# An attention kernel's probabilities-times-values product split into bf16 parts, and its projection batched by four row chunks

## The reference

```python
h = jnp.einsum('bse,end->bsnd', layernorm(x), proj_weight)     # 16 heads of 64
q = jnp.einsum('bsnd,ndh->bsnh', h, attn_weight)
scores = jnp.einsum('bsnh,brnh->bsnr', q, h) / head_dim
w = jax.nn.softmax(scores, axis=-1)
v = jnp.einsum('brnd,ndh->brnh', h, value_weight)
attn_out = jnp.einsum('bsnr,brnh->bsnh', w, v)
x = x + attn_out.reshape(b, s, -1) @ out_w.T + out_b
x = x + ffn(layernorm(x))      # gated, quantised weights and activations
```

## Time and profile before

| | us |
|---|---|
| time before, median of 2 runs | 8653.41 (8594.0 and 8712.82) |
| the profiled execution | 8581.15 |
| its span (slowest core, core 7) | 8579.6 |
| the eight cores' spans | 8538.1 to 8579.6 |
| mean granted TensorE clock of the cores | 0.771 to 0.775 of full |
| busy: PE, DVE, ACT | 5091.8, 2980.7, 1585.7 |

### The profile page before, as it was taken

How to read it: one execution, slowest core, us unless ns; L and a number is a source line. 1 busy time by engine, 2 the same in 40 slices (tenths; PEclk the granted TensorE clock), 3 DMA queues, 4 the chain that set the end, 5 groups by cost and what they waited for, 6 DMA issues and landing times.

```text
span 8579.6 us, 85041 instructions; the slowest of 8 cores (8538.1 to 8579.6 us)
## 1 busy us (share of the span) xinstructions
PE 5091.8 (59%) x26150; PEld 2254.4 (26%) x26150; DVE 2980.7 (35%) x7376; ACT 1585.7 (18%) x2602; POOL 88.2 (1%) x134
## 2 busy tenths in 40 slices
PE   0016668778778766668788687785344454353453
PEld 0015522222222215522222222122223232232232
DVE  5666631111111126631211212113543434435434
ACT  0000023333333320023233233231000000000000
POOL 0000000000000000000000000000000000000000
PEclk9997778888888887779889888786656666566566
DMA  8741100000000001100000000003334443343343
GB/s 273 234 143 35 33 7 2 4 2 2 4 2 1 2 19 35 36 9 1 5 2 1 5 2 1 2 1 67 66 80 83 74 89 65 68 94 69 74 89 69
DMA packets 837267, 396.21 MB, mean 46 GB/s; under 512 B 803939, under 2 KB 804067, under 8 KB 830692
## 3 DMA queue, kind: packets, MB, share of 16 engines
q1 hardware_dynamic: 827044, 353.00, 17.7%
q0 software_dynamic: 9792, 37.78, 1.2%
HBM read 352.95 MB, written 33.55 MB: 45 GB/s over the span
## 4 chain that ended last, share of the span: by engine, by line
PE 55%; DVE 23%; DMA 8%; issue 7%; DVEq 6%; ACT 0%; SPq 0%; POOLq 0%; ACTq 0%; POOL 0%
PE pb_av L718 23%; PE pb_s L735 10%; PE pb_av L464 6%; PE pb_av L843 3%; PE pf_d L1364 3%; PE pf_u L1191 2%; PE pf_g L1186 2%; PE pf_d L1191 2%; PE pf_d L1186 2%; DMA f_wd<-wdq 2%; DVE ln_lo L481 2%; DVE ln_hi L479 2%; DVE f_guq L1337 1%; DVE f_gr L1328 1%; DVE f_mx L1214 1%
## 5 line engine op out<-in xcount | busy, mean ns | idle before, releaser
L759 ACT ACTIVATE w<-pb_s,cbias 128x512 f32<-128x512 f32 x2048 | 1296.8, 684 | 1397.2 <-PE pb_s L735 1396.7
L768 DVE RECIPROCAL rr_t<-pb_av 1x512 f32<-1x512 f32 x64 | 210.1, 3320 | 2848.3 <-PE pb_av L718 2848.3
L718 PE MATMUL pb_av<-w,vA 128*65 128x512 f32 x2048 | 1125.4, 632 | 0.0
L718 PE MATMUL pb_av<-w,vB 128*65 128x512 f32 x2048 | 1055.5, 597 | 0.0
L1364 PE MATMUL pf_d<-f_guq,f_wd 128*128 128x256 bf16 x2048 | 299.0, 321 | 642.2 <-DVE f_guq L1337 542.9
L735 PE MATMUL pb_s<-q_hi,h_hi 64*128 64x512 bf16 x2048 | 439.2, 400 | 72.0 <-ACT w L759 71.5
L718 PEld LDWEIGHTS pb_av<-w,vB 128*65 128x65 f32 x2048 | 287.3, 140 | 617.5 <-issue 617.5
L735 PE MATMUL pb_s<-q_lo,h_hi 64*128 64x512 bf16 x2048 | 432.0, 393 | 0.0
L735 PE MATMUL pb_s<-q_hi,h_lo 64*128 64x512 bf16 x2048 | 431.2, 392 | 0.0
L1364 PEld LDWEIGHTS pf_d<-f_guq,f_wd 128*128 128x128 bf16 x2048 | 232.6, 115 | 710.2 <-issue 652.1
L1186 PE MATMUL pf_g<-f_xqf,f_wg 128*128 128x256 bf16 x1024 | 204.1, 366 | 276.3 <-DVEq L1219 267.2
(11 more groups left out here) (211 smaller groups left out, 5911.2 us busy)
## 6 DMA issues: line engine op xcount, KB each, us to landing
f_wg<-wgq SPq DMA_DIRECT2D x256, 256.0 KB, 3.3
f_wu<-wuq SPq DMA_DIRECT2D x256, 256.0 KB, 3.9
f_wd<-wdq SPq DMA_DIRECT2D x64, 1024.0 KB, 8.1
wraw<-wgT SPq DMA_DIRECT2D x16, 2048.0 KB, 10.1
wraw<-wuT SPq DMA_DIRECT2D x16, 2048.0 KB, 10.0
wraw<-wdT SPq DMA_DIRECT2D x64, 512.0 KB, 4.3
xa<-x_full SPq DMA_DIRECT2D x64, 512.0 KB, 3.8
x_tm<-x_full SPq DMA_DIRECT2D x16, 512.0 KB, 13.6
```

The source lines that it names most:

```text
L718: last = te.matmul(pb_av[2 + hidx][0:65, 0:512], vb[:, rc * 66:rc * 66 + 65], w32[:, wofs:wofs + 512], start=(rc == 0), stop=(rc == NRC - 1))
L759: a_e.inc(sc.activation(w32[:, slot:slot + 512], pb_s[hidx][:, 0:512], AFT.Exp, bias=cbias[:, hidx:hidx + 1], scale=1.0 / 64))
L768: v.reciprocal(rr_t[64:65, hidx * 512:(hidx + 1) * 512], pb_av[2 + hidx][64:65, 0:512])
```

## The change

Three edits.

- **AV in bf16 pairs.** vA and vB become bf16 pairs vA_hi, vA_lo, vB_hi, vB_lo: the V stage casts, drains and subtracts, with a one in the hi part's column 64 and a zero in the lo part's. Each exp tile (w32) is split by DVE into w_hi and w_lo, and AV is three bf16 matmuls per head in the place of one f32 matmul. AV waits for DVE's split (`v_w`) where it waited for the exp (`a_e`); the exp's wait for its slot is now on the split of rc - 2 (`v_w`) and no longer on its AV.
- **The projection of h takes four row chunks at once.** ln_hi and ln_lo hold four chunks. The PE does the transposes of four chunks and then 96 matmuls of 512 columns; the split of the first chunk of the next four waits for the whole projection. The h split handles 512 columns at a time and stands, in DVE's order, after the split of the second chunk of the next four.
- The buffer of the squares (xsq) exists once, and ACT drains after each Square.

```diff
-        vA = asb("vA", [128, NRC * 66], F32)
-        vB = asb("vB", [128, NRC * 66], F32)
+        vA_hi = asb("vA_hi", [128, NRC * 65], BF16)
+        vA_lo = asb("vA_lo", [128, NRC * 65], BF16)
+        vB_hi = asb("vB_hi", [128, NRC * 65], BF16)
+        vB_lo = asb("vB_lo", [128, NRC * 65], BF16)
...
-            xsq = hsb("xsq", [128, 2 * E], F32)
+            xsq = hsb("xsq", [128, E], F32)
             lnt = hsb("lnt", [128, E], F32)
-            ln_hi = hsb("ln_hi", [128, E], BF16)
-            ln_lo = hsb("ln_lo", [128, E], BF16)
+            ln_hi = hsb("ln_hi", [128, 4 * E], BF16)
+            ln_lo = hsb("ln_lo", [128, 4 * E], BF16)
...
                 a_sq.inc(sc.activation(
-                    xsq[:, (rc % 2) * E:(rc % 2 + 1) * E],
+                    xsq[:, 0:E],
                     xa[:, (rc % 2) * E:(rc % 2 + 1) * E], AFT.Square,
                     accum_out=stat[:, c + 0:c + 1]))
+                sc.drain()
...
-            def emit_pj(te, rc):
-                v_ls.w(te, bvls + 8 * rc + 8)
+            def emit_pj(te, rcq):
+                v_ls.w(te, bvls + 32 * rcq + 32)
                 for lc in range(4):
-                    pid = rc * 4 + lc
+                    pid = rcq * 4 + lc
...
                             last = te.matmul(
-                                pp[:, 0:128],
+                                pp[:, 0:512],
                                 wop[:, ic * 512 + lc * 128:ic * 512 + (lc + 1) * 128],
-                                rop[:, ic * 128:(ic + 1) * 128],
+                                rop[:, ic * 512:(ic + 1) * 512],
                                 start=first, stop=(wop is pw_lo and ic == 7))
...
-                    if ib == 0 and rc >= 1:
-                        t_pj.w(v, btpj + 4 * rc)
+                    if ib == 0 and rc >= 4:
+                        t_pj.w(v, btpj + 4 * (rc // 4))
                     src = ltp[ib % 4][:, 0:128]
-                    v.tensor_copy(ln_hi[:, ib * 128:(ib + 1) * 128], src)
+                    dst = ib * 512 + (rc % 4) * 128
+                    v.tensor_copy(ln_hi[:, dst:dst + 128], src)
                     v.drain()
...
-                    dst = lc * 4096 + rc * 128
-                    v.tensor_copy(h_hi[:, dst:dst + 128], pp[:, 0:128])
+                    dst = lc * 4096 + rcq * 512
+                    v.tensor_copy(h_hi[:, dst:dst + 512], pp[:, 0:512])
                     v.drain()
                     v_he.inc(v.tensor_tensor(
-                        h_lo[:, dst:dst + 128], pp[:, 0:128],
-                        h_hi[:, dst:dst + 128], ALU.subtract))
+                        h_lo[:, dst:dst + 512], pp[:, 0:512],
+                        h_hi[:, dst:dst + 512], ALU.subtract))
                     v.drain()
...
-                for rc in range(NRC + 1):
-                    if 1 <= rc:
-                        emit_pj(te, rc - 1)
-                    if rc < NRC:
-                        emit_lt(te, rc)
+                v_af.w(te, prev_af_h)
+                for rc in range(NRC):
+                    if rc >= 4 and rc % 4 == 0:
+                        emit_pj(te, rc // 4 - 1)
+                    emit_lt(te, rc)
+                emit_pj(te, NRC // 4 - 1)
...
-                for rc in range(NRC + 2):
+                for rc in range(NRC + 3):
...
-                    if 2 <= rc < NRC + 2:
-                        emit_he(v, rc - 2)
+                    if rc >= 6 and (rc - 6) % 4 == 0:
+                        emit_he(v, (rc - 6) // 4)
...
                 for rc in range(NRC):
                     t_v.w(v, btv + rc + 1)
-                    for (hp, vb) in ((0, vA), (64, vB)):
+                    o = rc * 65
+                    for (hp, vh, vl) in ((0, vA_hi, vA_lo), (64, vB_hi, vB_lo)):
                         pav = pb_av[(0 if hp == 0 else 2) + rc % 2]
-                        v.tensor_copy(vb[:, rc * 66:rc * 66 + 64], pav[:, 0:64])
-                        v.memset(vb[:, rc * 66 + 64:rc * 66 + 65], 1.0)
+                        v.tensor_copy(vh[:, o:o + 64], pav[:, 0:64])
+                        v.memset(vh[:, o + 64:o + 65], 1.0)
+                        v.drain()
+                        v.tensor_tensor(vl[:, o:o + 64], pav[:, 0:64],
+                                        vh[:, o:o + 64], ALU.subtract)
+                        v.memset(vl[:, o + 64:o + 65], 0.0)
                     v_ve.inc(v.drain())
...
                     def emit_av(rc):
                         for hidx in range(2):
-                            a_e.w(te, bae + 2 * rc + hidx + 1)
+                            v_w.w(te, bvw + 2 * rc + hidx + 1)
...
-                            vb = [vA, vB][hidx]
-                            last = te.matmul(
-                                pb_av[2 + hidx][0:65, 0:512],
-                                vb[:, rc * 66:rc * 66 + 65],
-                                w32[:, wofs:wofs + 512],
-                                start=(rc == 0), stop=(rc == NRC - 1))
+                            vh, vl = [(vA_hi, vA_lo), (vB_hi, vB_lo)][hidx]
+                            o = rc * 65
+                            for k, (vv, ww) in enumerate(
+                                    ((vh, w_hi), (vh, w_lo), (vl, w_hi))):
+                                last = te.matmul(
+                                    pb_av[2 + hidx][0:65, 0:512],
+                                    vv[:, o:o + 65],
+                                    ww[:, wofs:wofs + 512],
+                                    start=(rc == 0 and k == 0),
+                                    stop=(rc == NRC - 1 and k == 2))
                         t_av.inc(last)
...
                             if rc >= 2:
-                                t_av.w(sc, btav + rc - 1)
-                            elif btav > 0:
-                                t_av.w(sc, btav + rc - 1)
+                                v_w.w(sc, bvw + 2 * rc - 2)
+                            elif bvw > 0:
+                                v_w.w(sc, bvw + 2 * rc - 2)
...
+                @blk.vector
+                def _(v):
+                    for rc in range(NRC):
+                        for hidx in range(2):
+                            a_e.w(v, bae + 2 * rc + hidx + 1)
+                            slot = (2 * (rc % 2) + hidx) * 512
+                            v.tensor_copy(w_hi[:, slot:slot + 512],
+                                          w32[:, slot:slot + 512])
+                            v.drain()
+                            v.tensor_tensor(w_lo[:, slot:slot + 512],
+                                            w32[:, slot:slot + 512],
+                                            w_hi[:, slot:slot + 512], ALU.subtract)
+                            v_w.inc(v.drain())
```

More of the change, by code:

```diff
@@ L338, in emit_hbuild @@
             prev_nm = v_nm.n
+            prev_af_h = v_af.n
             @blk.sync
@@ L475, in emit_ls, with emit_he @@
                     t_lt.w(v, btlt + tid + 1)
-                    if ib == 0 and rc >= 1:
-                        t_pj.w(v, btpj + 4 * rc)
+                    if ib == 0 and rc >= 4:
+                        t_pj.w(v, btpj + 4 * (rc // 4))
                     src = ltp[ib % 4][:, 0:128]
-                    v.tensor_copy(ln_hi[:, ib * 128:(ib + 1) * 128], src)
+                    dst = ib * 512 + (rc % 4) * 128
+                    v.tensor_copy(ln_hi[:, dst:dst + 128], src)
                     v.drain()
                     v_ls.inc(v.tensor_tensor(
-                        ln_lo[:, ib * 128:(ib + 1) * 128], src,
-                        ln_hi[:, ib * 128:(ib + 1) * 128], ALU.subtract))
+                        ln_lo[:, dst:dst + 128], src,
+                        ln_hi[:, dst:dst + 128], ALU.subtract))
                     v.drain()
-            def emit_he(v, rc):
+            def emit_he(v, rcq):
                 for lc in range(4):
-                    pid = rc * 4 + lc
+                    pid = rcq * 4 + lc
                     t_pj.w(v, btpj + pid + 1)
                     pp = pb_av[lc]
-                    dst = lc * 4096 + rc * 128
-                    v.tensor_copy(h_hi[:, dst:dst + 128], pp[:, 0:128])
+                    dst = lc * 4096 + rcq * 512
+                    v.tensor_copy(h_hi[:, dst:dst + 512], pp[:, 0:512])
                     v.drain()
                     v_he.inc(v.tensor_tensor(
-                        h_lo[:, dst:dst + 128], pp[:, 0:128],
-                        h_hi[:, dst:dst + 128], ALU.subtract))
+                        h_lo[:, dst:dst + 512], pp[:, 0:512],
+                        h_hi[:, dst:dst + 512], ALU.subtract))
                     v.drain()
@@ L523, in _ @@
                         emit_ls(v, rc - 1)
-                    if 2 <= rc < NRC + 2:
-                        emit_he(v, rc - 2)
+                    if rc >= 6 and (rc - 6) % 4 == 0:
+                        emit_he(v, (rc - 6) // 4)
             @blk.vector
             def _(v):
-                v_he.w(v, bvhe + NRC * 4)
```

(7 more changed lines are left out.)

## The result

The changed kernel takes 9035.9 us (median of 11 runs, 9017.6 to 9103.1). The kernel before, on the same chips, took 8714.5 us (median of 10, 8586.0 to 9043.1). In some executions the cores of one die show a lower mean granted clock and take up to several per cent longer, and the ratios leave those out. The ratio of the changed kernel to the one before is 1.053, with a 95% interval from 1.049 to 1.057: slower. The profiled execution took 9028.1 us where that of before took 8581.2, so 447 us more; the prediction's sum was 380 more.

What follows compares the result with a forecast made beforehand. PE was taken to bound the attention loop before, at 2.62 us a step, and DVE after. Loops +128, V stage +154 and h build +98 gave +380 on 8581.2, 8961; forecast 8970 us, range 8790 to 9250.

Steps and rivals of the forecast that it cites:

- rival 1: Likeliest: DVE sets the attention loop, and the h build and V stage lose too; 8850 to 9120 us, chance 0.74.
- tile, step of the loop: Attention loop: DVE splits one head's exp tile in 1.38 us, two tiles a step, 2.76 us against PE's 2.62 before.
- loops: All 32 attention loops: 4.0 us longer each, +128 us; bounds -16 to +352.
- V stage: V stage: each head's copy becomes cast, drain, subtract; 1.17 us a chunk for 0.565, +154 us, bounds 128 to 192.
- h build: Two h builds: DVE work hidden under projections comes out; 68.3 us per four chunks for 61.4, +98 us in all.
- The gap of 0.19 us: Attention loop: DVE's time for drain with increment and wait after each subtract; 0.19 us taken, bounds 0.12 to 0.30.
- rivals 1 and 3: DVE sets the loop (0.74), against a wait that costs nothing, tile 1.31 us, other stages low, 8750 us (0.08).
- About 0.9 us lost: Start of each attention loop: DVE out of tiles while the half-clock PE delays the third scores and exp, about 0.9 us.
- the lump of h splits: h build: four h splits after each projection over four chunks, together 6.4 us on DVE, under nothing.
- Rival 2: Attention loop: PE clock falls because PE now idles in each step; about 9650 us if in half the steps, chance 0.14.
- Rival 4: Attention loop: cast and subtract overlap, tile under 1.1 us, PE sets the pace; 8250 us, chance 0.04.
- The ring: Attention loop: dependency circle PE, ACT, DVE, 2.52 us against DVE's 2.76, so at least 0.2 us to spare.

Runs made afterwards that it cites:

- inter2: Changed kernel with the projection over two row chunks, cut into four parts placed between the transposes: 8770.2 us, ratio to before 1.019.
- regroup: Changed kernel with DVE doing both casts, one drain, both subtracts, one drain per step, AV of both heads waiting for that: 9169.4 us, ratio to before 1.066.
- lag2: Changed kernel with AV two steps behind the scores instead of one, three slots per tile: 9042.5 us, ratio to before 1.048.
- combo: Kernel before with bf16 pairs for head A only, projection over two chunks interleaved with transposes, V stage over four chunks: 8202.1 us, ratio 0.952.
- no_lo: Changed kernel without w_lo: DVE only casts each exp tile, AV is two matmuls a head: 8316.3 us, ratio to before 0.963.
- hb_only: Kernel before with the h build's edits alone, V stage and attention loop as before: median of six 9079.9 us, no ratio can be given.
- regroup_lag2: Changed kernel with both casts, drain, both subtracts, drain per step, and AV two steps behind the scores: 8643.6 us, ratio to before 1.000.
- mix34: Kernel before with bf16 pairs for head A always and for head B on even row chunks only: 8732.5 us, ratio 1.013.

## Why the prediction was right, point by point

The forecast was 8970 us, with rival 1 the likeliest; measured was 9036, inside the range and inside rival 1's own (8850 to 9120). The mechanism was right in all three parts. The terms:

| term | forecast | measured |
|---|---|---|
| tile, step of the loop | 1.38, 2.76 us | 1.38, 2.76 us |
| loops | +128 us (4.0 x 32) | +166 us (5.2 x 32) |
| V stage | +154 (1.17 us a chunk) | +164 (1.19) |
| h build | +98 (quad 68.3) | +104 (quad 68.29) |
| sum on the profiled execution | +380 | +447, of which 13 not traced |

- **The gap of 0.19 us.** Taken from V's row, "a drain with an increment and one satisfied wait", and exact. That one choice decided between rivals 1 and 3. Rows of the same sequence on the same engine, in another stage and at another tile size, carried over.
- **Loops: the term that fell furthest short**, by 38 of the 67 us that were missing in all, or 1.2 us a loop. Three things make it up. "About 0.9 us lost" at the start was 1.57 us in the loop shown and 1.15 in the mean. I had the sequence right but gave the third exp too early: from the start of the third scores to the end of their first exp I took 1.8 us (1149.9 to 1151.7), though my own half-clock terms, 1.52 + 0.70, give 2.2; the trace has 1217.09 to 1219.4, 2.3. Some 0.5 us a loop are idle stretches of DVE in the steady part, mostly of a few tenths (1244.68: 0.54 us, put down to an exp that had ended 0.7 us before); what causes them stays open. The last 0.35 is no slowness of the change: I compared with one loop of before, 86.18 us, and the mean of its 32 is 85.84.
- **V stage.** 1.19 for 1.17: an extra gap of 0.2 before head B's cast came in some chunks (0.20 at 1162.20), not in others. The upper bound was +0.75 a chunk; +0.64 came.
- **h build.** The quad came out to a hundredth, partly by luck: the projection was 22.3 us and not 23.3, since the clock rose after some seven of the 96 matmuls and not twelve, and the chunks without a projection took 10.7 us and not 10.51. The argument held: the lump of h splits lies under nothing. inter2 tested it by giving the cover back, and the loss turned into a gain.
- **DVE's share.** Forecast near 87% busy, measured 80% (48.10 of 60 us): I had counted the drain between cast and subtract as busy. The step doesn't hang on it.
- **Rival 2, the clock.** The prediction put 0.14 on it, with the output projection's row against it (76% busy at 0.98). The loop is at 1.00 with PE 84% busy by the records (50.26 of 60 us), some 75% by spacing. The row was the right guide. The oscillation from micro-idles between matmul groups that the Trainium skill ("TensorE: Matmul & The Clock Gate", A second HAM failure mode) describes does not show in this loop, whose clock stays at 1.00.
- **Rival 4** (tile under 1.1 us) was refuted by the timeline; regroup shows how near it lay: with the drain shared by two tiles DVE's step is 2.32 us, 1.16 a tile.
- **The ring.** That it has room in the change was right: lag2, which gives it a whole step more, changes nothing in the steady loop, and regroup, which makes it longer by a tile, loses at once. How much room, the runs do not say; 0.2 us was an estimate.
- **Feed-forward.** Left untouched in the sum; from the attention's last write into x_tm to the end it is 2741.5 us against 2739.5.

## What to carry to other kernels

Price a change of precision by what the splitting costs on the engine that must do it, per tile with its drain and its gap, and compare that with the step of the engine that it relieves; here 2 x 1.38 us on DVE replaced a PE step of 2.62, while one tile (half of the trade) fitted under it and paid. When a long matmul group is made longer and rarer, ask what lay under each of the short ones: cut it into parts and put them between the steps of the work that must be covered. When two limits lie close together (DVE's sum at 2.76 us, the ring at an estimated 2.52), an edit that eases one at the other's cost loses and one that opens the slack one does nothing, so try them together before dropping either.

## What the runs showed of the hardware that I had not expected

**A third level of the granted clock, 0.81.** Ten of the thirteen traces have stretches at it, with matmuls of 512 columns 0.26 us apart where they are 0.215 at 1.00; those of before, the change and combo have none. Core 1 of no_lo, PE:

```profile
1221.38 0.44 PE L732 MATMUL pb_av<-w_hi,vB_hi 128*65 128x512 bf16 x1
1221.65 0.43 PE L732 MATMUL pb_av<-w_hi,vB_lo 128*65 128x512 bf16 x1
```

It is not tied to the bf16 products. hb_only has the attention loop of before, f32 matmuls and all, and core 0 has whole loops at 0.81 in a trace where core 4 has every loop at 1.00. A window of core 0:

```profile
4245.00:4330.00 85.00, 85.00 (x270) 20.50 (x269) 0.00 (x0) 33.88 (x55) 0.00 (x0) 0.81 0.00 0
```

What it costs depends on which engine sets the pace. In hb_only, where PE does, the scores there come 3.16 us apart (4300.12, 4303.28) for 2.62, and a loop takes up to 103.2 us for 85.3. In regroup_lag2, where DVE's and PE's sums lie close, a step takes 2.60 us for 2.32. In the change's own loop it costs nothing; the same stretch of inter2 on core 4, then on core 6:

```profile
5100.00:5130.00 30.00, 25.34 (x132) 7.81 (x131) 24.35 (x44) 13.71 (x22) 0.00 (x0) 1.00 0.00 1
5100.00:5130.00 30.00, 29.93 (x132) 8.51 (x130) 24.37 (x44) 13.49 (x23) 0.00 (x0) 0.81 0.00 1
```

Both cores make the same 132 matmuls and 44 DVE instructions in 30 us.

The cores 2b and 2b + 1 show the level at nearly the same times of their spans, the two pairs of a die at different ones. In inter2, cores 4 and 5 have all of it between 640 and 1163 us, cores 6 and 7 between 4675 and 5197: 522 us from the first to the last, both times. In mix34 it is 1288 to 1448 and 7995 to 8154. Equal lengths at shifted times are what one would see if the two pairs do not start together and the level falls while both are dense at one moment. Times here count from each core's own start and no row gives the shift, so this is inferred, not shown. It has a consequence for reading: the same window on two cores need not be the same moment.

The Trainium skill ("TensorE: Matmul & The Clock Gate", Part 1, on a peak-current limiter) says that a die is taken to 13/16 of the clock once three of its cores run dense matmuls. The level agrees, 0.81, and the shifted pairs would fit it; the moments at which three cores were dense cannot be read from these traces.

**Loads do not average over steps.** mix34's three tiles in two steps took 5.25 us and regroup's steps alternate between 2.32 and 3.38, though each engine's work was under 2.4 a step. With one step of lookahead in the queues, the longest path through every single step counts. A second step of lookahead brought regroup's mean from 2.85 us to 2.32 (regroup_lag2, clock 1.00).
